# Reordering the last two rounds of an attention kernel, and moving three waits and loads to where their data is used

## The reference

```python
xn = _layernorm(x)
x = x + _L0_attn_ref(xn, ...) + _L0_ffn_ref(xn, ...)

# _L0_attn_ref, "local": 16 query heads, 4 key/value heads, RMS norm and rotary embedding on q and k
mask = causal | (jnp.abs(idx[:, None] - idx[None, :]) > 64)
attn = softmax(where(mask, -1e4, q @ k.T * scale))
out = (attn @ v) @ Wo.T + bo

# _L0_ffn_ref, "routed": each token picks one of 16 heads' keys and values
gating = softmax(x @ W_gate.T); idx = argmax(gating); top1_val = max(gating)
k_shared = sum_h(indicator * k)             # one key head of 32 for all query heads
v_shared = sum_h(indicator * top1_val * v)
att = softmax(causal(q @ k_shared.T / sqrt(32)))
y = att @ v_shared
```

## Time and profile before

| | |
|---|---|
| median of 3 runs | 690.89 us (690.03 to 694.57) |
| the profiled execution | 694.83 us |
| its span, first to last instruction | 693.0 us |
| PE busy | 647.3 us, 93% |
| DVE / POOL / ACT busy | 72% / 64% / 52% |
| mean granted TensorE clock | 0.986 |

### The profile page before, as it was taken

How to read it: one execution, slowest core, us unless ns; L and a number is a source line. 1 busy time by engine, 2 the same in 40 slices (tenths; PEclk the granted TensorE clock), 3 DMA queues, 4 the chain that set the end, 5 groups by cost and what they waited for, 6 DMA issues and landing times.

```text
span 693.0 us, 19466 instructions
## 1 busy us (share of the span) xinstructions
PE 647.3 (93%) x7432; PEld 510.8 (74%) x7432; DVE 496.6 (72%) x1328; ACT 363.0 (52%) x906; POOL 442.7 (64%) x368
## 2 busy tenths in 40 slices
PE   3678999999999899999898789999999999999997
PEld 3567788888788788887787567777767777777775
DVE  3966867677777786797674258887888787879544
ACT  4445434554347145265435335565665665666675
POOL 3975674937393753786394237687868777778740
PEclk9999999999999999999999889999999999999999
DMA  8523222231141222311212561141314031402011
GB/s 303 192 58 103 69 62 83 85 110 55 47 112 53 70 69 74 95 46 56 77 47 70 154 180 47 50 109 49 108 46 113 28 108 49 110 28 86 4 32 33
DMA packets 65133, 56.61 MB, mean 82 GB/s; under 512 B 6672, under 2 KB 49040, under 8 KB 65040
## 3 DMA queue, kind: packets, MB, share of 16 engines
q1 hardware_dynamic: 62896, 54.45, 26.7%
q10 hardware_dynamic: 2144, 0.93, 0.5%
HBM read 37.20 MB, written 17.89 MB: 80 GB/s over the span
## 4 chain that ended last, share of the span: by engine, by line
PE 75%; DVE 10%; POOL 5%; ACT 4%; issue 3%; DMA 2%; ACTq 1%; DVEq 0%; POOLq 0%
PE gemm L904 15%; PE s_ps L1021 11%; PE od_ps L1066 11%; PE st_ps L1052 10%; PE gemm L990 6%; PE od_ps L1080 5%; PE win L964 3%; PE gemm L900 3%; PE win L949 2%; PE s_ps L1090 2%; ACT p_loc L1461 2%; DMA rope_t<-rope 2%; DVE l_sum L1237 2%; PE av L976 2%; DVE l_max L1228 1%
## 5 line engine op out<-in xcount | busy, mean ns | idle before, releaser
L904 PE MATMUL gemm<-w_tok,xt 128*128 128x512 f32 (+1 forms) x768 | 184.7, 382 | 4.6 <-DVE g_exp L1151 2.0
L904 PEld LDWEIGHTS gemm<-w_tok,xt 128*128 128x128 f32 x768 | 130.9, 192 | 28.7 <-DVE g_exp L1151 3.0
L1291 DVE CUSTOM_DVE_ANT_0 s_ps<-s_ps,x_ln 128x512 f32<-128x512 f32 (+3 forms) x224 | 127.6, 620 | 30.3 <-PE s_ps L1021 29.9
L1021 PE MATMUL s_ps<-k_stack,w_tok 96*128 96x512 f32 (+2 forms) x336 | 103.2, 388 | 0.9 <-DVE x_res L1254 0.8
L1052 PE MATMUL st_ps<-w_tok,k_stack 98*128 98x512 f32 x288 | 100.2, 416 | 1.6 <-ACT p_loc L1507 1.6
L1507 ACT ACTIVATE p_loc<-st_ps 128x512 f32<-128x512 f32 x144 | 77.2, 599 | 39.5 <-PE st_ps L1052 31.0
L1601 POOL TENSOR_TENSOR rope_b<-qkv,sin_t 128x128 f32<-128x128 f32 (+1 forms) x32 | 27.5, 880 | 78.5 <-DVE qkv L1203 78.4
L1021 PEld LDWEIGHTS s_ps<-k_stack,w_tok 96*128 96x128 f32 x336 | 55.9, 190 | 28.3 <-DVE picked_fk L1291 11.1
L1461 ACT ACTIVATE p_loc<-win,l_max 128x96 f32<-128x96 f32 x256 | 61.1, 392 | 20.6 <-DVE l_max L1228 20.5
L1625 POOL TENSOR_TENSOR p_loc<-p_loc,l_rec 128x1536 f32<-128x1536 f32 x16 | 44.1, 2758 | 30.2 <-DVE l_rec L1240 30.2
L1507 ACT ACTIVATE p_loc_t<-st_ps 128x512 f32<-128x512 f32 x96 | 52.4, 599 | 20.5 <-PE st_ps L1052 20.0
(11 more groups left out here) (172 smaller groups left out, 1299.8 us busy)
## 6 DMA issues: line engine op xcount, KB each, us to landing
w_tok<-q_parts SPq DMA_DIRECT2D x96, 128.0 KB, 2.8
q_parts<-qt SPq DMA_DIRECT2D x120, 64.0 KB
x_ln<-x SPq DMA_DIRECT2D x8, 512.0 KB, 4.6
x_res<-x SPq DMA_DIRECT2D x16, 256.0 KB, 2.8
partial<-x_res SPq DMA_DIRECT2D x16, 256.0 KB, 2.8
w_tok<-partial SPq DMA_DIRECT2D x8, 512.0 KB, 5.7
raw<-w_tok SPq DMA_DIRECT2D x3, 1024.0 KB, 13.1
v_win<-v_rows SPq DMA_DIRECT2D x64, 48.0 KB, 2.2
```

What stands on the lines that cost most here:

```text
L904: i = e.matmul(g[:, 0:cols], xs[l][:, k, a * P:(a + 1) * P], w_tok_p[r][:, k, c0:c0 + cols], start=first, stop=last)
L1021: e.matmul(s_ps[bank][:, 0:cols], q_op[b][0:HALVES, i, h, :], k_stack[0:HALVES, b * S + c0:b * S + c0 + cols], start=True, stop=True).then ...
L1291: e.tensor_tensor_reduce(out=s[:, 0:cols], in0=s[:, 0:cols], in1=causal[:, S - width + c0:S - width + c0 + cols], scale=1.0, scalar=dst if ...
```

## The change

`LAST_UNITS` goes, and one list now gives the products of both last rounds, mixed: the local queries q(7,0) and q(7,1) stand ahead of most of the routed products of rounds 6 and 7. The planner gets two rules that keep `kvg`, `fk` and `fv` behind the pick of the tile before. DVE's wait for the mask moves from the step `routed_rooms` to the first row maxima, where the mask is read. The queries of unit 1 no longer wait for the last two chunks, but for the chunk that they hold; for this the last two chunks get store semaphores of their own, `q_last0` and `q_last1`. Their loads stand two quarters each behind the steps `qt` 2 and `qt` 3 of round 7. The two `partial_load`s of units 0 and 1 move behind their unit's first output row, and row 4.

```diff
-LAST_UNITS = [("kvg", 0), ("q", 0), ("fk", 0), ("kvg", 1), ("q", 1), ("fk", 1), ("fv", 0), ("fv", 1), ("qt", 0),
-              ("qt", 1), ("qt", 2), ("qt", 3)]
+LAST_PRODUCTS = [(6, "kvg", 0), (6, "q", 0), (6, "fk", 0), (6, "kvg", 1), (6, "fv", 0), (6, "qt", 0), (6, "q", 1),
+                 (7, "kvg", 0), (6, "fk", 1), (6, "fv", 1), (7, "q", 0), (7, "kvg", 1), (6, "qt", 1), (7, "q", 1),
+                 (7, "fk", 0), (6, "qt", 2), (7, "fk", 1), (6, "qt", 3), (7, "fv", 0), (7, "fv", 1), (7, "qt", 0),
+                 (7, "qt", 1), (7, "qt", 2), (7, "qt", 3)]
...
-        if (n, c) == (ROUNDS - 1, 1):
-            for quarter in range(2, 4):
-                do("q_load", 0, 0, 0, quarter)
-        if (n, kind, c) == (ROUNDS - 1, *LAST_UNIT):
-            for quarter in range(4):
-                do("q_load", 1, 0, 1, quarter)
+        if n == ROUNDS - 1 and c:
+            u, quarters = ((0, (2, 3)), (1, (0, 1)), (1, (2, 3)))[c - 1]
+            for quarter in quarters:
+                do("q_load", u, 0, u, quarter)
+                p.q_lands[u, quarter] = p.now + Q_LANDS * (1 + quarter % 2)
...
+            if u == 0 and i % PART == 0:
+                self.do("partial_load", i // PART, 0, i // PART)
...
-            elif step == "routed_rooms":
-                lane.wait_ge(*M["masked"].of("all"))
-
...
                     lane.wait_ge(*(M["r_mm"].of(u - 1) if u > 1 else M["fk_dup"].of((ROUNDS - 1, 1))))
+                    lane.wait_ge(*M["masked"].of("all"))
...
                 elif u < B:
-                    lane.wait_ge(*M["gemm_mm"].of((ROUNDS - 1, *LAST_UNIT)))
+                    lane.wait_ge(*M["gemm_mm"].of((ROUNDS - 1, "fv", 1)))
+                    lane.wait_ge(*M["q_stored0"].of((ROUNDS - 1, 0)))
+                else:
+                    lane.wait_ge(*M["q_stored1"].of((ROUNDS - 1, 1)))
                     for s in range(2):
-                        lane.wait_ge(*M[f"q_stored{s}"].of((ROUNDS - 1, 2 + s)))
-                else:
+                        lane.wait_ge(*M[f"q_last{s}"].of(LAST_CHUNKS[s]))
                     lane.wait_ge(*M["rst_mm"].of((u - 2, PRODUCTS.index((2 * c + 1, 2 * c)))))
```

More of the change, by code:

```diff
@@ L76 @@
 VALUES_AT_ONCE = 4
+Q_LANDS = 4.0
 ROOM = 0.1
@@ L178, in make_plan @@
     p.turned, p.transposed, p.projected, p.fk_stacked = set(), set(), set(), -1
-    p.q_kept, p.av_free, p.rooms = -1, 0.0, False
+    p.q_kept, p.av_free, p.rooms, p.picked = -1, 0.0, False, set()
+    p.q_lands = {}
     win_free = [0.0] * HKV
@@ L252, in ready @@
                 return None
+            if n and kind == "kvg" and ("fv", n - 1, a) not in p.picked:
+                return None
+            if kind in ("fk", "fv") and n + a and (kind, *((n, 0) if a else (n - 1, 1))) not in p.picked:
+                return None
             return max(*whats, piece_ready[piece])
@@ L287, in take_routed @@
             do("fv_out", n, a)
+            p.picked.add(("fv", n, a))
             yield 0, [("A", 0.3)]
@@ L292, in take_routed @@
         do("fk_lo", n, a)
+        p.picked.add(("fk", n, a))
         yield 0, [("V", 0.3)]
@@ L444, in make_plan @@
     for n in range(ROUNDS):
-        p.products.extend(product(n, unit) for unit in (UNITS if n < ROUNDS - 1 else LAST_UNITS))
+        if n < ROUNDS - 2:
+            p.products.extend(product(n, unit) for unit in UNITS)
+    p.products.extend(product(n, (kind, a)) for n, kind, a in LAST_PRODUCTS)
     p.run(when)
     do("routed_banks")
-    for b in range(B):
-        do("partial_load", b, 0, b)
     routed_stage(p)
@@ L466, in __init__ @@
         self.p, self.now, self.busy, self.do = p, p.now, p.busy, p.do
-        self.q_ready = {(u, c): 0.0 for u in range(B) for c in range(IT // 2)}
+        self.q_ready = {(1, c): p.q_lands[1, c] for c in range(IT // 2)}
         self.row_ready = {0: p.now}
@@ L682 @@
     "xt_mm xt_hi xt_lo gemm_mm gemm_read kv_r sq_r rms_r rope_ab rope_sum rope_r "
-    "g_sum_r g_top_r picked_fk picked_fv fk_hi fk_lo fk_dup fv_out qt_hi q_stored0 q_stored1 fk_mm fk_out "
+    "g_sum_r g_top_r picked_fk picked_fv fk_hi fk_lo fk_dup fv_out qt_hi q_stored0 q_stored1 q_last0 q_last1 fk_mm fk_out "
     "v_pad v_out0 v_out1 v_in0 v_in1 q_t_mm q_t_r k_t_mm k_t_r s_mm s_max p_exp masks l_sum l_rec p_r pt_mm "
@@ L840, in qt_of, with stored @@
         return qt[part][:, c % 2, :]
+    def stored(n, c):
+        return M[f"q_last{c % 2}" if (n, c) in LAST_CHUNKS else f"q_stored{c % 2}"]
     def raw_of(n):
@@ L1514, in scalar_program @@
                     for s in range(2):
-                        lane.wait_ge(*M[f"q_stored{s}"].of(LAST_CHUNKS[s]))
+                        lane.wait_ge(*M[f"q_last{s}"].of(LAST_CHUNKS[s]))
                 if i >= 2:
@@ L1701, in sync_program @@
                         e.dma_start(dst, qt_of(part, n, c)[:, a * P:(a + 1) * P].bitcast(F32)).then_inc(
-                            *M[f"q_stored{c % 2}"].did((n, c), inc=16))
+                            *stored(n, c).did((n, c), inc=16))
             elif step == "res_load":
```

## The result

| | before | changed |
|---|---|---|
| median of 13 runs each, same chip | 692.16 us (689.99 to 696.55) | 699.03 us (695.90 to 700.58) |
| profiled execution / its span | 694.83 / 693.0 us | 700.19 / 698.9 us |
| mean granted clock in it | 0.986 | 0.971 |

The ratio is 1.008, with a 95% interval of 1.0059 to 1.010. So the change costs 4 to 7 us, where I had forecast a gain of 1.3, with 684.8 to 692.9 us as the range.

A forecast was written before the change was run, and what follows sets the result against it. Bound: ACT's routed start waits for the last `partial` store on SP's nearly full queue. PE's chain gains 6.0 us, the queue lets 1.3 through, mask, loads and clock add nought: 694.83 to 693.5, median 689.6, range 684.8 to 692.9 us.

The forecast's parts named there:

- Local queries first: Tile (7,1)'s local attention starts earlier, so PE's chain up to the last residual gains 6.0 us (4 to 7.5).
- The key's low part: DVE's low part of tile (7,1)'s key ends with POOL's scaling at 371.0, not after the 0.52 us median.
- The mask: DVE's wait for POOL's mask cost between 0 and 4.41 us; moving it gives no gain beside the 6.0.
- the SP queue: SP issues the last `partial` store at 399.8 to 401.3, landing 3.1 later; ACT's start gains 1.3 of 6.0 us.
- the SP queue does not bind: At the seam, ACT starts when the store at 396.2 lands, 399.0: 6.0 us gained, 684.9 us; chance 0.20.
- the queue slows down: SP's alternating stores and loads issue slower, last store up to 4.1 us later: 691.9 to 695.0 us; shared chance 0.18.
- new stalls: Reordering makes PE wait in rounds 6 and 7: up to 3 us more, 691 to 693; shared chance 0.18.
- The clock: PE's granted clock around ACT's routed start: nought taken, with -2.6 and +2 us kept as limits.
- The `partial` loads: Moved behind output rows, their transfers hide under routed work: cost nothing, gain nothing, at most 1 us.

The follow-up runs named there:

- new order alone, ACT waits later: Kernel before with only the new product order of the last two rounds, and ACT's wait for the last partial stores moved to the first output row: 1.0021.
- changed, ACT waits later: Changed kernel with ACT's wait for the last partial stores moved to unit 1's first output row: 689.66 us, 0.9947.
- second wait filled: Changed kernel with 22 useless PE products put into PE's 6.3-us wait for ACT, ahead of the fifth key scores: 694.84 us, 1.0014.
- both waits filled: Changed kernel with 22 useless PE products in each of PE's two seam waits, for unit 1's queries and for ACT: 697.26 us, 1.0061.

## Why the prediction was wrong

- **Local queries first: right.** Exponentials of (7,1) until 376.6 predicted, 375.6 aligned measured; POOL's scaling at 380.7, measured 380.4; last residual at 396.2, measured 394.3. PE's chain gained 7.8 us, above the 6.0 and just above its 4 to 7.5, for nothing. Most of the excess lies behind POOL's scaling: 13.9 us from its start to the last residual, before 15.5. Before, the clock was 0.91, 0.50 and 0.73 in the windows from 388 to 394; now it is 1.00 there.
- **The key's low part: right.** It took 1.36 us and ended at 372.20, as POOL did at 372.15, and PE waited 2.46 for it.
- **The mask: right.** I had its worth alone between 0 and 4.41 us, and no gain beside the 6.0. Alone it makes PE's chain 3.4 us shorter (aligned). In the new order it makes none that shows: the last output product begins at 390.6 aligned with the mask's wait in its old place (new order alone, ACT waits later) and in its new one (changed, ACT waits later). What I had not foreseen is that alone, with ACT's wait where it was, it gains nothing.
- **The step that failed: the SP queue, "ACT starts at 402.9 to 404.4, middle 403.7".** The mechanism was the right one, also that it starts at 378.7 (378.5 aligned) and that the last store goes out late; its size was not. The 42 DMAs ahead of that store took 24.4 us (380.58 to 404.99) and not 21.1 with at most 1.5 for one slow group: 24 loads 13.2 for 11.0, 16 stores 9.4 for 8.3. One load alone took 1.9 us; what made it slow is not shown. Then the store took 5.09 us to land and not 3.1. Against the middle, 2.3 us of issue and 2.0 of landing make, with 0.1 for the way to ACT, the 4.4 by which ACT's start, 408.05 aligned, missed. Alike in size, the landing is the plainer mistake: I had written that more loads were in flight, and then took a value from the rows of three stores behind only 12 loads, ahead of which the queue had stood idle for 3.8 us. The rival "the SP queue does not bind" is out: SP never stood idle. The rival "the queue slows down", at a chance of 0.18 with the new stalls, was what happened, at a price above its own 691.9 to 695.0; it had only the stores slow, but the loads lost more, and it left the landing at 3.1.
- **Overlooked: PE's wait for unit 1's queries.** I had PE do "their first few row maxima and scores" at 396. They need a load that is on the same queue, and PE stood 5.6 us. In the changed kernel ACT was later still; with ACT freed it is what bounds.
- **The clock, "I take nought": wrong in the way it was counted.** I asked where the low stretch of before would fall. At the seam it is not a stretch of its own: in these traces it follows PE's idle time. 7 us of idle time had been predicted, and a low clock behind it should have been. The kernel with its second wait filled shows 4.2 us to be had (284.6 for 288.8). Before paid 3.4 of them already, so it adds only 0.8 in the profiled pair.
- **New stalls in rounds 6 and 7: no idle time added, but one wait counts.** From 300 to 378.4 PE is busy 74.13 us, before 72.51, partly because the clock is slower (0.98, before 1.00). PE's 2.46 us for the key's low part now lie on the chain to the first store of the queue, and the clock behind them is 0.50 from 372 to 374 and 0.66 from 374 to 376:

```profile
370.92 1.29 DVE fk_stack L1209
...
372.91 3.97 PE gemm L919 x12
```

  In PE's timeline these twelve matmuls take 4.32 us, and 3.02 in the trace with both waits filled, whose clock stayed full there. In that trace the queue starts at 377.7 aligned, and in the nine other traces with the new order at 378.5 to 380.0. So that 378.7 was met is in part luck: its working had no low clock in it.
- **The `partial` loads: nothing**, as predicted; no wait for them shows.

Of the 6.9 us between the medians the profiled pair explains 3.8 as the change's own: 3.0 of ACT's start and 0.8 of clock behind it, against a forecast of -1.3 and nought. The rest, up to 3 us, stays open: only one execution of each has a trace. That the mean clock of the 13 changed runs is 0.971 to 0.982, while that of the 118 runs of the kernel before beside the experiments was 0.978 to 0.993, points to the clock, but is no proof. One place where it can be lost is the low stretch ahead of the queue, by which the queue's start moved over 2.3 us between the traces of the new order. Open, too, is why both waits filled (1.0061) did worse than the second alone (1.0014), though in the two traces the routed stage took the same 284.6 us: eight of the eleven executions took 3 to 7 us longer than the one with the trace, and none of these has a trace.

## What to carry to other kernels

Before one chain is made shorter, list every wait at the seam behind it, and for each the queue position of what releases it; a gain is worth only what the last of them lets through. Here the cheapest edit was not to reorder anything but to move ACT's wait to where its data matters (0.9981, with an interval that reaches 1.0001), and the mask's wait as well (0.9935, 0.65% off). Count the landing of a transfer by what is in flight when it is issued, and count idle time of PE twice, for itself and for the slow clock behind it; a shorter chain in front of an unmoved wait can therefore gain nothing, or make a kernel slower.

## What the runs showed of the hardware

- The last three stores of 256 KB landed 2.8 to 3.6 us after their issue in the kernel before, behind 12 loads of 128 KB issued without a gap. The last two landed after 4.9 and 5.1 us in the changed kernel, where 42 DMAs without a gap, 24 of them such loads, stood ahead, and the last after 4.1 us when ACT issued it.
- Issuing one of these 24 loads took SP 352 ns at the least, 427 in the median and 1941 at the longest.
- All these programs have the same order in the first 50 us, where their executions come apart; the first row maxima of the routed stage then started anywhere from 299.75 to 302.30 us. The mean clock of the first 50 us, 0.86 to 0.97 over these traces, does not tell it alone: 302.11 us came with 0.97, and 300.93 with 0.90.
- 22 idle-time products took 5.2 to 5.3 us at full clock, and 6.3 where they began at the lower one.
